# Four row tiles as two jobs of two, attention's weights centred, and new orders on every engine

## What is computed

```
x = x + attn_a(layernorm(x))   # linear attention, 16 heads of 8
x = x + ffn(layernorm(x))      # relu squared, 128 -> 512 -> 128, then 5 steps of a spiking unit
x = x + attn_b(layernorm(x))   # one head, rotary positions, masked softmax over 2048 keys
x = x + ffn(layernorm(x))      # the same ffn

layernorm(x) = (x - mean(x)) / sqrt(var(x) + 1e-5)       # no gain, no offset

attn_a: q, k, v = x Wqkv^T;  q, k = elu(q) + 1, elu(k) + 1
        kv = sum over all rows of k v^T, ksum = sum of k (for each head)
        out = (q kv) / (q ksum + 1e-6);  out Wproj^T + bproj
```

## Time and profile before

| | |
|---|---|
| median of 3 runs | 191.12 us (190.76 to 191.35) |
| the profiled execution | 190.59 us |
| its span on the core | 188.4 us |
| PE busy | 177.7 us of the span |
| DVE busy | 149.4 us |
| ACT busy | 111.2 us |
| POOL busy | 48.6 us |

### The profile page before, as it was taken

One profiled execution on the slowest core, in us unless ns is written; L12 is line 12 of the kernel. 1 busy time (PEld: TensorE's weight loads), 2 busy tenths in 40 slices (PEclk: granted clock), 3 DMA queues, 4 the chain that ended last, 5 costly groups with the idle time before them and its releaser, 6 DMA issues.

```text
span 188.4 us, 3886 instructions
## 1 busy us (share of the span) xinstructions
PE 177.7 (94%) x1270; PEld 157.6 (84%) x1270; DVE 149.4 (79%) x472; ACT 111.2 (59%) x257; POOL 48.6 (26%) x65
## 2 busy tenths in 40 slices
...
DMA packets 9825, 5.96 MB, mean 32 GB/s; under 512 B 447, under 2 KB 9422, under 8 KB 9806
## 3 DMA queue, kind: packets, MB, share of 16 engines
...
...
## 4 chain that ended last, share of the span: by engine, by line
PE 74%; DVE 14%; issue 4%; ACT 3%; DMA 2%; POOL 1%; DVEq 0%; ACTq 0%; POOLq 0%
PE bank_o L1117 15%; PE bank_m L1047 12%; PE bank_p L1105 7%; PE bank_s L907 6%; PE bank_s L909 5%; PE bank_s L908 5%; PE bank_h L907 3%; PE bank_h L909 3%; PE bank_h L908 3%; PE bank_m L942 3%; PE bank_h L978 2%; DVE rsin L384 2%; DVE xn L699 2%; DMA id_sb<-in_ident 2%; DVE stat L677 1%
## 5 line engine op out<-in xcount | busy, mean ns | idle before, releaser
L1117 PE MATMUL bank_o<-vone,pt 128*128 128x128 f32 x272 | 35.9, 274 | 0.0
L1117 PEld LDWEIGHTS bank_o<-vone,pt 128*128 128x128 f32 x272 | 34.3, 191 | 0.9
L1047 PE MATMUL bank_m<-wd,hid 128*128 128x128 f32 x256 | 32.2, 276 | 0.6 <-DVE y L769 0.4
L1047 PEld LDWEIGHTS bank_m<-wd,hid 128*128 128x128 f32 x256 | 30.9, 192 | 2.0 <-DVE y L769 0.8
L473 POOL TENSOR_SCALAR veps<-mom 128x4 f32<-128x4 f32 (+2 forms) x19 | 7.1, 371 | 96.3 <-DVE mom L681 96.0
L611 ACT ACTIVATE relu<-bank_h 128x512 f32<-128x512 f32 (+1 forms) x40 | 20.0, 511 | 11.0 <-PE bank_h L909 9.5
L666 ACT COPY pt<-bank_p 128x512 f32<-128x512 f32 (+3 forms) x31 | 16.1, 531 | 13.1 <-PE bank_p L1105 12.9
L789 DVE SCALAR_TENSOR_TENSOR spiked<-y,spiked 128x512 bf16<-128x512 f32 (+1 forms) x36 | 22.1, 613 | 0.6
L907 PE MATMUL bank_s<-kh,qh 128*128 128x512 f32 (+3 forms) x43 | 17.7, 412 | 0.9 <-ACT vone L646 0.4
L677 DVE BATCH_NORM_STATS2 stat<-xs 128x6 f32<-128x128 f32 x64 | 14.2, 281 | 3.5 <-DMA xs<-in_x 3.4
L657 ACT ACTIVATE kphi<-kphi,negm 128x1024 f32<-128x1024 f32 (+4 forms) x12 | 11.3, 938 | 7.0 <-DVE negm L866 7.0
...
## 6 DMA issues: line engine op xcount, KB each, us to landing
...
hid<-in_w_qkv ACTq DMA_DIRECT2D x1, 192.0 KB, 4.1
```

Source lines behind the costliest of these rows:

```text
L1047: last = nc.tensor.matmul(MB[:, C * t:C * t + C], hid[:, j % 2, m, P * t:P * t + P], wd[:, m, :], start=(m == 0), stop=(m == M - 1))
L1117: last = nc.tensor.matmul(O[:, C * (i % TG):C * (i % TG) + C], pt[:, n % 3, P * b:P * b + P], v[:, k, :], start=(k == 0), stop=(k == i))
```

## The change

Normalisation 0 gets five jobs, the first group being cut in two jobs of two tiles, so x is loaded in five pieces. The weight of attn_a is centred by a new step `centre-0` on PE, in bank P1, from which `w_hi-0` (ACT) and `w_lo-0` (now DVE) split it. `norm` is then a multiplication by `rstd` alone: on DVE one instruction for a whole job, and a second form on ACT, which does jobs 0, 1 and 2, one instruction for each tile. The warm-up has 8 matmuls. `lane_columns` puts the halves of group 0 side by side in the slot that a whole group has, and `rows_turned` lets `kv` begin when its own two tiles are there. All four lists of `PLAN` are written in another order, and some steps change the engine.

```diff
-NORM_JOBS = [GROUPS, MLP_JOBS[0], GROUPS, MLP_JOBS[1]]
+NORM_JOBS = [[(0, 2), (2, 2)] + GROUPS[1:], MLP_JOBS[0], GROUPS, MLP_JOBS[1]]
+J0 = len(NORM_JOBS[0])
-WARM_UP = 16
+WARM_UP = 8
...
-keep_warm-3 turn-0-0 keep_warm-4 kv-0-0 q-0 turn-0-1 kv-0-1 turn-0-2 kv-1-0 q-1 turn-0-3 kv-1-1 kv-2-0 q-2 acc-0
+centre-0 turn-0-0 turn-0-1 keep_warm-3 kv-0-0 q-0 turn-0-2 keep_warm-4 kv-0-1 turn-0-3 kv-1-0 q-1 kv-1-1 turn-0-4
...
-w_hi-0 hi-0-0 kv_exp-0-0 hi-0-1 q_exp-0 kv_exp-0-1 hi-0-2 kv_exp-1-0 q_exp-1 hi-0-3 kv_exp-1-1 q_exp-2 kv_exp-2-0
+norm-0-0 w_hi-0 hi-0-0 norm-0-1 hi-0-1 norm-0-2 kv_exp-0-0 hi-0-2 q_exp-0 kv_exp-0-1 hi-0-3 kv_exp-1-0 q_exp-1
...
-centre ids rstd-0-0 rstd-0-1 w_lo-0 rstd-0-2 bias-0 rstd-0-3 rstd-1-0 bias-1 sq-0-0 bias-2 sq-1-0 vnext_zero rstd-1-1
+centre rstd-0-0 rstd-0-1 rstd-0-2 rstd-0-3 rstd-0-4 bias-0 ids bias-1 rstd-1-0 vnext_zero bias-2 rstd-1-1 sq-1-0
...
+        def rows_turned(t):
+
+            return lo_ready[0], next(k for k, (a, b) in enumerate(NORM_JOBS[0]) if a + b > t) + 1
...
-            for g in range(G):
-                sp.dma_start(xs[:, TG * g:TG * g + TG, :], x_t[:, TG * g:TG * g + TG, :]).then_inc(x_in[g], 16)
+            for j, (t0, nt) in enumerate(NORM_JOBS[0]):
+                sp.dma_start(xs[:, t0:t0 + nt, :], x_t[:, t0:t0 + nt, :]).then_inc(x_in[j], 16)
...
+                    for t in range(nt):
+                        k = t0 + t
+                        last = nc.scalar.activation(xn[:, j % 2, t, :], xs[:, k, :], ACT.Copy, scale=rstd[:, n, k:k + 1])
+                    last.then_inc(*one(done["norm", n, g]))
...
-                    for t in range(nt):
-                        k = t0 + t
-                        last = nc.vector.tensor_scalar(xn[:, j % 2, t, :], xs[:, k, :], mom[:, n, k, 0:1],
-                                                       rstd[:, n, k:k + 1], ALU.subtract, ALU.mult)
-                    last.then_inc(*one(done["norm", n, g]))
+                    nc.vector.tensor_tensor(
+                        xn[:, j % 2, 0:nt, :], xs[:, t0:t0 + nt, :],
+                        rstd[:, n, t0:t0 + nt].unsqueeze(2).to_broadcast([P, nt, C]), ALU.mult).then_inc(
+                            *one(done["norm", n, g]))
...
-                    pe.wait_ge(lo_ready[0], g + 1)
+                    pe.wait_ge(*rows_turned(TG * g + 2 * pr + 1))
```

More of the change, by code:

```diff
@@ new lines @@
+kv_exp-1-1 hi-0-4 kv_exp-2-0 q_exp-2 kv_exp-2-1 kv_exp-3-0 kv_exp-3-1 q_exp-3 w_hi-1 w_hi-2 aT_copy-0 hi-1-0 aT_copy-1
+hi-1-1 relu-0-0 relu-0-1 sq-0-0 sq-0-1 relu-0-2 relu-0-3 sq-0-2 aT_copy-2 relu-1-0 relu-1-1 hi-1-2 sq-1-1 relu-1-2
+relu-1-3 relu-2-0 hi-1-3 full-1-3 relu-2-1 relu-2-2 sq-2-1 relu-2-3 sq-2-3 aT_copy-3 relu-3-0 relu-3-1 sq-3-0 hi-2-0
+sq-3-1 relu-3-2 relu-3-3 qkv_copy-0-0 hi-1-4 qkv_copy-0-1 qkv_copy-0-2 qkv_copy-0-3 relu-4-0 relu-4-1 y-3 qk_hi-0-0
+qk_hi-0-1 relu-4-2 hi-2-1 relu-4-3 sq-4-2 e-0-0 qkv_copy-1-0 qkv_copy-1-1 qkv_copy-1-2 qkv_copy-1-3 e-1-0 pt_copy-1-0
@@ L159 @@
-k_phi-1-0 q_phi-0 lo-0-3 q_phi-1 k_phi-1-1 q_phi-2 k_phi-2-0 k_phi-2-1 k_phi-3-0 k_phi-3-1 diag q_phi-3 heads-0
-heads-1 w_lo-1 w_lo-2 x1-0 stats-1-0 lo-1-0 stats-1-1 heads-2 lo-1-1 x1-1 sq-0-2 stats-1-2 y-0 spike-0-0 spike-0-1
-x1-2 lo-1-2 heads-3 sq-1-3 spike-0-2 stats-1-3 spike-0-3 spike-0-4 sq-2-2 xf-0 y-1 spike-1-0 spike-1-1 spike-1-2
-spike-1-3 spike-1-4 xf-1 stats-2-0 spike-2-0 spike-2-1 lo-2-0 x1-3 spike-2-2 stats-1-4 lo-1-4 spike-2-3 spike-2-4
-cos-0 sin-0 rot-0-0 rot-0-1 xf-2 stats-2-1 qk_lo-0-0 qk_lo-0-1 lo-2-1 score_copy-0-0 score_copy-1-0 spike-3-0
@@ L179 @@
-spike-10-1 spike-10-2 spike-10-3 spike-10-4 xf-10
+stats-0-0 stats-0-1 stats-0-2 w_lo-0 lo-0-0 stats-0-3 lo-0-1 stats-0-4 norm-0-3 lo-0-2 k_phi-0-0 q_phi-0 norm-0-4
+lo-0-3 k_phi-0-1 k_phi-1-0 k_phi-1-1 q_phi-1 lo-0-4 k_phi-2-0 q_phi-2 k_phi-2-1 k_phi-3-0 k_phi-3-1 q_phi-3 diag
+heads-0 heads-1 w_lo-1 w_lo-2 x1-0 stats-1-0 lo-1-0 heads-2 lo-1-1 stats-1-1 sq-0-3 x1-1 stats-1-2 y-0 spike-0-0
+spike-0-1 x1-2 lo-1-2 heads-3 sq-1-3 sq-2-0 stats-1-3 sq-2-2 spike-0-2 spike-0-3 spike-0-4 y-1 spike-1-0 xf-0
```

172 lines of the change are left out of this document (89 added, 83 removed).

## The result

| | before | after |
|---|---|---|
| median of 4 runs each, side by side | 191.23 us (190.76 to 191.35) | 192.69 us (192.46 to 192.97) |
| ratio, 95% interval | | 1.0078 (1.0053 to 1.0103) |
| profiled execution, its span | 190.59, 188.4 us | 192.8, 191.0 us |
| `centre-1` starts (24.41 in the chain) | 24.25 | 27.13 |
| last DVE instruction starts | 186.13 | 188.74 |

The forecast was 190.3 us and faster; the time is 2.4 us above it and outside the range. The changed kernel also scatters more.

What follows compares the result with a forecast made beforehand. PE was taken as the bound (busy 177.7 of 188.4 us), with DVE setting the pace from 60 to 100. The start's 0.8 gain took the execution from 190.59 to 189.8; plus half a microsecond, 190.3 us, range 188.8 to 191.9.

Steps and rivals of the forecast that it cites:

- On DVE `w_lo-0` 0.55 and `lo-0-0` 0.41 end at 8.15, in time: Start, DVE: the weight and group 0 low parts are ready before the first `kv`, forecast at 9.1 us.
- the walk: Step-by-step timing of the new lists through the start with durations of before; `centre-1` at 23.65, about 0.8 us gained.
- the 0.95 gained at `q-0`: Start, PE: `q-0` begins at 9.8 us instead of 10.75, when `lo-0-1` is done.
- the new order hangs group 1 on the last load: Start: x's last piece lands at 10.8, `lo-0-2` ends at 13.45, so PE waits 0.5 us before `kv-1-0`.
- From `q-0` to `centre-1`: PE from 9.8 to 23.65: 0.5 us wait before `kv-1-0`, then 10.2 us of work through `acc-3`.
- The eight warm-up matmuls taken away cost and give nothing by themselves: Start, PE: removing them is worth zero, because PE waits for `w_qkv` anyway.
- PE's slower level: Rival, start: PE stays at 1.2 GHz until `q-0` is done, 1.5 us lost against 0.8 gained, 191.8; chance 0.1.
- The rule of the Trainium skill on transposes: Start, PE: transposes do not count as busy like matmuls; by it the clock stays slow and the time is 191.8.
- The `bias` steps lie in POOL's free time: Start, POOL: the bias additions were given no cost.
- the orders behind `acc-3` are worth nothing: After the start: reordered steps gain zero, within 0.5 us either way at `tqk` and `s`; the 0.8 passes on.
- the rival of a new wait: Rival, 100 to 180 us: PE waits 1.5 us or more for `pt_copy` steps now on DVE, 191.9; chance 0.08.
- The sum: Whole kernel: span 188.4 less 0.8 is 187.6, profiled execution 189.8, forecast median 190.3 us, -0.4%.

Runs made afterwards that it cites:

- i2: The changed kernel itself, unchanged, run again for its spread and a second trace; median 192.87 us, ratio 1.0016.
- h1: The changed kernel with three small loads (`heads`, `w_proj`, `b_proj`) issued by SP behind the mask instead of by ACT; median 189.83 us, ratio 0.9935.
- h4: h1 with `bias-0` waiting for the last `k_phi` and `bias-1` moved behind `rstd-1-0` on POOL; median 188.97 us, ratio 0.9881.
- e1: The changed kernel with `w_lo-0` and `lo-0-0` ahead of `stats-0-2` on DVE; median 191.72 us, ratio 1.0023.
- f3: The kernel before the change with 8 warm-up matmuls instead of 16; median 191.43 us, ratio 0.9992.
- i1: The changed kernel with only the `b_proj` broadcast load issued by SP behind the mask instead of by ACT; median 190.41 us, ratio 0.9937.
- e2: The changed kernel with 11 more keep-warm matmuls on PE, between and behind the first transposes; median 191.66 us, ratio 1.0030.
- e3: The changed kernel with both the DVE move of e1 and the 11 keep-warm matmuls of e2; median 191.69 us, ratio 1.0025.
- f1: e3 with POOL's `bias-0` and `bias-1` waiting until `acc-3` is done; median 190.94 us, ratio 0.9980.
- g3: f1 without `keep_warm-4`, with all engines' lists behind `acc-3` taken from the kernel before; median 192.34 us, ratio 1.0030.

## Why the prediction was wrong

**The step that failed** is the sentence "On DVE `w_lo-0` 0.55 and `lo-0-0` 0.41 end at 8.15, in time". I had the durations and not the wait ahead of them: `stats-0-2` stands in front, and I never costed the landing of its piece, only that of the last. At that step the walk put nothing for x. The same walk did say that each queue place matters (the last piece "about 0.5 later"); for tiles 4 to 7 the move is from second place, landing at 5.5, to third, at 8.0, and of the 0.95 gained at `q-0` it makes a loss. So the dependence that I looked for was the right kind, on the wrong piece: to "the new order hangs group 1 on the last load" belonged that it hangs group 0 on the third. The last piece was not the bound in the first profile: the last `stats` start at 11.58 with no wait. Where the third piece came early it was: in i2 the last `stats` wait for x until 10.97 (said: 10.8) and `lo-0-2` ends at 13.44 (said: 13.45).

| step | predicted | changed | h1 (loads moved) |
|---|---|---|---|
| `w_hi-0` done | 7.2 | 6.32 | 6.53 |
| `lo-0-0` done | 8.15 | 10.16 | 8.16 |
| `kv-0-0` | 9.1 | 10.22 | 8.44 |
| `q-0` | 9.8 | 11.72 | 9.71 |
| `norm-0-3` on DVE | 0.69 | 0.69 | 0.69 |
| `centre-1` | 23.65 | 27.13 | 23.96 |
| `centre-1` to the last DVE instruction | as before, 161.9 | 161.6 | |

With the piece in time (h1) `lo-0-0`, `q-0` and `centre-1` come within 0.3 us of the walk, `w_hi-0` and `kv-0-0` 0.7 earlier. In the changed kernel `w_qkv` landed at 4.2 and not at 5.3, and `centre-0` took 1.02 and not 1.4, so it ended at 5.71 and not at 6.7; that is why `kv-0-0` comes earlier than 9.1 wherever `lo-0-0` lets it. That h1's `centre-1` is so near is in part luck: no wait for the last piece (`kv-1-0` at 12.87, said: 13.45), and in its place the time that POOL takes from DVE. So is the time of i2, 190.16 against the forecast 190.3: its `centre-1`, 24.45, is 0.8 later than forecast.

**From `q-0` to `centre-1`** the prediction has 13.85 us, h4 13.40, h1 14.25 and the changed kernel 15.41. Read as steps: 0.85 for POOL's `bias` (h4 to h1), 1.16 more with the slower level (h1 to the changed kernel, which fits the 1.0 between e1's two sets of spans). These are single traces, and the split between the two is worked out from them, not measured by itself.

**"The eight warm-up matmuls taken away cost and give nothing by themselves"** holds in the median in the old order (f3). In the new one the slower level comes in many executions and goes with about 1 us; the changed kernel with 16 warm-up matmuls was not run, so how much of that the eight account for is open. The rival "PE's slower level" said 191.8, deciding when it "lasts beyond `kv-0-0`". In the changed kernel's first trace it came otherwise than the rival had it: `keep_warm-3` and `kv-0-0` ran at the faster level, and it fell behind the wait for `lo-0-0`, so that `q-0` and `keep_warm-4` ran at 1.2 GHz. In i1's trace it came as the rival had it, with `keep_warm-3`, `kv-0-0` and `q-0` slow behind short transposes with gaps. I gave it 0.1 because a gap of 0.54 had done no harm; the pauses are 1.05 ahead of the second transposes and, in the changed kernel, 1.64 ahead of `kv-0-0`. That the level costs time was right; alone it is not the whole loss. The rule of the Trainium skill on transposes (TensorE: Matmul & The Clock Gate, PE-mode transpose), weighed there, is neither shown nor refuted by these runs: e2 and e3 put matmuls between the transposes and shorten the pause with one edit.

**"The `bias` steps lie in POOL's free time"** is true of POOL and wrong for the kernel: they slow DVE beside them, 0.75 us from e3 to f1 and 0.86 from h1 to h4.

**That the orders behind `acc-3` are worth nothing** was right, by 161.6 against 161.9 and by g3. (The trace has 13 of the `pt_copy` on DVE, 9 before; the rival of a new wait counted 12. No such wait came.)

**The sum** was made against a span of 188.4; the span of most executions of the kernel before is 189.5. I had seen the half microsecond between that execution and the median and put it on top. It could not tell me where a usual execution is longer, and the walk compared the new start with that of a short one.

**Open** is why the kernel before loses nothing in the median with eight warm-up matmuls, and why the third piece lands early in some executions and 2 us later in others. Shown is that moving the broadcast away brings the last piece of x from 9.5 to 11.0 us down to 7.3 to 7.9, takes 2.5 us off the median, and leaves spans of 187.9 to 189.8 (i1) where they were 188.3 to 192.5 (i2).
